# Row statistics one batch ahead, and V pieces 0 and 1 in the places of K pieces 6 and 7, in a gated cross-attention and mixture-of-experts block

## The chip, the cores and the metric

One core of a Trainium2 chip runs the whole program. The metric is device time in microseconds (us) of one execution, as the median of several runs. Engines are named PE (TensorE, matrix products), DVE (VectorE), ACT (ScalarE), POOL (GpSimd) and SP (SyncE, which here issues most DMAs).

## What is computed

x has 8 batches of 512 rows of 256, the context 8 batches of 1601 rows of 256.

```python
x = x + tanh(g_xattn) * xattn(layernorm(x), ctx, ctx)
x = x + tanh(g_ffn) * ffn(layernorm(x))

# xattn: 16 heads of 16; note the softmax over the queries (axis 2)
qh, kh, vh = heads(q @ Wq.T), heads(k @ Wk.T), heads(v @ Wv.T)
attn = softmax(einsum('bhnc,bhlc->bhnl', qh * 256 ** -0.5, kh), axis=2)
attn = attn / attn.sum(-1, keepdims=True)
out = einsum('bhnl,bhlc->bhnc', attn, vh) ... @ Wo.T

# ffn: top 2 of 8 experts, 256 -> 1024 (gelu) -> 256, weighted by the normalised router probabilities
```

## The kernel before

The program has two stages: attention with routing, batch by batch, and then the experts over 71 blocks of 128 routed rows. The change touches the first alone.

**Steps and units.** The 16 heads form four groups (g) of four, the 1601 context rows 13 tiles of up to 128 (the last has 65). A step s is one tile of one group, 52 steps a batch; its two units (p = 0, 1) have two heads each. For each unit PE makes scores, transposed, with the context rows on partitions and 512 queries in the columns (L732, `unit_scores`), DVE takes the negated maximum over the queries (L1114), ACT makes two exponentials with their sums (L934). There are three slots of scores in PSUM (`SLOTS`): a unit's scores wait for the exponentials of the unit three before. Per step DVE then inverts the four sums (L1100, `reciprocals`), POOL scales the tile of V by them (L1337), and PE multiplies three steps later (L745, `weigh`). At a turn of groups DVE takes the accumulator (L1104).

**Q and K in three parts.** Q and K are used in 16-bit parts: each projected piece is split into a high part (ACT, L870, `take`), a residual (DVE, L1009), a middle and a low part (POOL, L1389 and L1381, the low one a step later). The three parts of a piece lie in `parts`, a pair of buffers that pieces use in turn (`c % 2`), and SP stores them to DRAM (`store_parts`, Q on L445, K on L450). From there SP loads the stacks of a group of heads, 16 DMAs for each (`load_stacks`, L407 and L412). `ORDER` is the order in which the ten pieces of a batch are made and stored: K 0 to 7, then Q 0 and 1. K pieces 0 to 3 and Q 0 serve groups 0 and 1, K 4 to 7 and Q 1 groups 2 and 3. Before ACT writes a piece into its buffer it waits until the piece two before has been stored:

```python
wait(act, parts_stored[c % 2], (b * (CHUNKS // 2) + at // 2) * 16)   # at: the piece's place in ORDER
```

V pieces need none of this: ACT copies them once (L879) and DVE has no part in them.

**The order around the change.** The work beside the scores stands in tables by step (`FILL_AT`, for batch 0 `FIRST_BATCH_FILL_AT`): "next" pieces are projections of the batch after, "tail" those that finish the batch before (its last attention turn, the output projection, the routing), "cur" the batch's own. All share one PSUM bank, `spare`, so a piece starts on PE only when the one before has been taken. PE starts half of a K, Q or V piece a step early. ACT takes its part at the beginning of the step in front of the step's exponentials, DVE its part of Q and K at the end of the step. SP's program is one sequence: it waits for a piece's parts, issues, and goes on. `load_x` and `load_ctx` fetch x and the context two batches ahead, once their buffers are free (L461 after step 28, L466 after step 47).

**Statistics of x.** The layer norm of the next batch's x takes four row statistics on DVE (L1143, at `STATS_X`, steps 7 and 11 to 13), four aggregates (L1147, step 16), and POOL's normalising from step 17 (`CENTRE_X`). The statistics of x2 for the routing (L1133, L1137) stand at steps 10 to 12.

Of the kernel before, what the change touches and what calls it, by code (L numbers as in the profile page):

```python
# [41 lines left out]
KC = D // P  # L42
NT = N // P
LT = (L + P - 1) // P
GH = 4
G = H // GH
STEPS = G * LT
UNITS = 2 * STEPS
# [5 lines left out]
KCHUNK = 4  # L54
# [14 lines left out]


FILL_AT = {
    1: ("next", "k", 0), 3: ("next", "k", 1), 4: ("tail", "o_turn", 3), 5: ("tail", "attn_turn", 1),
    7: ("tail", "out_proj", 0), 9: ("tail", "out_proj", 1), 11: ("next", "k", 2), 13: ("next", "k", 3),
    15: ("next", "k", 4), 17: ("next", "k", 5), 18: ("cur", "o_turn", 0), 19: ("tail", "row_turn", 0),
    20: ("tail", "row_turn", 1), 22: ("tail", "logits", 0), 24: ("next", "k", 6), 26: ("next", "k", 7),
    27: ("next", "x_turn", 0), 28: ("next", "x_turn", 1), 30: ("next", "q", 0),
    32: ("next", "q", 1), 33: ("cur", "o_turn", 1), 35: ("next", "v", 0), 37: ("next", "v", 1), 38: ("tail", "prefix", 0),
    40: ("next", "v", 2), 42: ("next", "v", 3), 44: ("next", "v", 4), 46: ("next", "v", 5),
    47: ("next", "v", 6), 48: ("cur", "attn_turn", 0), 49: ("cur", "o_turn", 2),
}  # L80
# [5 lines left out]
FIRST_BATCH_FILL_AT = {  # L86
    1: ("cur", "own_v", 3), 3: ("cur", "own_v", 4), 5: ("cur", "own_v", 5), 6: ("cur", "own_v", 6),
    11: ("next", "k", 0), 13: ("next", "k", 1), 15: ("next", "k", 2), 17: ("next", "k", 3), 18: ("cur", "o_turn", 0),
    20: ("next", "k", 4), 22: ("next", "k", 5), 24: ("next", "k", 6), 26: ("next", "k", 7),
    27: ("next", "x_turn", 0), 28: ("next", "x_turn", 1), 30: ("next", "q", 0),  # L90
    32: ("next", "q", 1), 33: ("cur", "o_turn", 1), 35: ("next", "v", 0), 37: ("next", "v", 1), 39: ("next", "v", 2), 41: ("next", "v", 3),
    43: ("next", "v", 4), 44: ("cur", "o_turn", 2), 46: ("next", "v", 5), 47: ("next", "v", 6),
    48: ("cur", "attn_turn", 0),
}
# [7 lines left out]
LAG = 3  # L102
WARM_TURNS = 24
WARM_ROUTING, WARM_PLACED, WARM_EXPERTS, WARM_ROWS = 40, 60, 24, 18
ORDER = [KC + i for i in range(KC * KCHUNK)] + list(range(KC))
LOGITS = 22
ROUTE = 25
PLACE = 39
OUT = 9
STATS_X = (7, 11, 12, 13)  # L110
CENTRE_X = 17


class Iteration:
# [65 lines left out]
def wait_apart(eng, sem, value, passed):  # L180


    eng.wait_ge(sem, value)
    eng.sem_inc(passed, 1)
# [27 lines left out]
def attention_and_routing(nc, ctx, block, keep, x, ctx_t, g_xattn, g_ffn, wq_t, wk_t, wv_t, wo_t, router_t,  # L212
# [227 lines left out]
    def _(sp):  # L440
# [50 lines left out]
        def run(it):  # L491
            b = it.b
            if b == 0:

                sp.wait_ge(fill_taken, it.made("own_v", VF - 1))
                sp.dma_start(ctx_sb[:, :, :], ctx_rows[1]).then_inc(ctx_loaded, 16)
                stored_early(sp, ("q", 1), *(("k", i) for i in range(KCHUNK, 2 * KCHUNK)))
                load_stacks(0, 2)
            if it.cur and b > 0:

                wait(sp, scores_ready, b * UNITS)
                load_stacks(b, 3)
            if it.next:

                for g in range(G):
                    wait(sp, stack_in[g], stacks_by(b, g))
                for c in ORDER[0:KCHUNK]:
                    store_parts(it, c)
            if it.tail:
                sp.wait_ge(fill_taken, it.made("out_proj", 1))  # L510
                sp.dma_start(out_rows[b - 1], x2[:, :, :]).then_inc(x2_stored, 16)
            if it.next:
                for c in ORDER[KCHUNK:2 * KCHUNK]:
                    store_parts(it, c)
            if b == 0:
                load_stacks(0, 3)
            if it.cur:
                if it.tail:

                    wait_apart(sp, x2_stored, b * 16, passed_sp)  # L520
                    wait_apart(sp, rows_ready, 2 * b, passed_sp)
                sp.dma_start(x2[:, :, :], x_rows[b]).then_inc(x2_loaded, 16)
            if it.ahead:
                load_x(it)
            if it.next:
                stores = CHUNKS // 2 * 16
                store_parts(it, 0)
                wait_apart(sp, parts_stored[0], (b + 1) * stores, passed_sp)
                wait_apart(sp, parts_stored[1], (b + 1) * stores - 16, passed_sp)
                sp.wait_ge(scores_ready, b * UNITS + 2 * LT)  # L530
                load_stacks(b + 1, 0)
                store_parts(it, 1)
                wait_apart(sp, parts_stored[1], (b + 1) * stores, passed_sp)
                for g in range(1, G - 1):
                    sp.wait_ge(scores_ready, b * UNITS + (g + 1) * 2 * LT)
                    load_stacks(b + 1, g)
            if it.ahead:
                load_ctx(it)

# [39 lines left out]
    def _(pe):  # L579
# [63 lines left out]
        def fill(it, name, i, halves):  # L643
            b = it.b
            if 0 not in halves:
                pass
            elif name != "logits":

                wait(pe, fill_taken, it.made(name, i) - 1)
            if name == "x_turn":  # L650

                pe.wait_ge(xn_ready, 2 * (b + 2))
                mm = turn_x(spare, i)
            elif name == "q":
                mm = project_q(spare, i, halves)
            elif name == "k":
                if i == 0 and 0 in halves:
                    pe.wait_ge(ctx_loaded, (b + 1) * 16)
                mm = project_k(spare, i, halves)
            elif name in ("v", "own_v"):  # L660
                if (name, i) == ("own_v", len(EARLY_COPIED) - KC) and 0 in halves:

                    pe.wait_ge(early_copied, len(EARLY_COPIED))
                mm = project_v(spare, i, halves)
            elif name == "o_turn":

                pe.wait_ge(acc_taken, b * G + i + 1 if i < G - 1 else b * G)
                for t in range(NT):
                    mm = pe.transpose(spare[:, t * P:(t + 1) * P], o_acc[:, t * P:(t + 1) * P], ident[:, :])
            elif name == "attn_turn":  # L670
                for t in range(NT):
                    mm = pe.transpose(spare[:, t * P:(t + 1) * P], attn[:, t, i * P:(i + 1) * P], ident[:, :])
            elif name == "out_proj":
                if i == 0:
                    pe.wait_ge(wo_in, 32)
                for t in (2 * i + h for h in halves):
                    for k in range(KC):
                        mm = pe.matmul(spare[:, (t % 2) * D:(t % 2 + 1) * D], attn_t[:, k, t * P:(t + 1) * P],
                                       wo_sb[:, k, :], start=(k == 0), stop=(k == KC - 1))
            elif name == "row_turn":  # L680

                pe.wait_ge(rows_ready, 2 * b)
                for t in range(NT):
                    mm = pe.transpose(spare[:, t * P:(t + 1) * P], routed_rows[:, 0, t, i * P:(i + 1) * P], ident[:, :])
            elif name == "logits":
                for t in range(NT // 2, NT):
                    for k in range(KC):
                        mm = pe.matmul(spare[:, t * E:(t + 1) * E], row_t[:, k, t * P:(t + 1) * P],
                                       router_sb[:, k, :], start=(k == 0), stop=(k == KC - 1))
            elif name == "pads":  # L690
                mm = pe.matmul(spare[:, 0:E], ones[:, :], seen[:, :], start=True, stop=True)
            else:

                pe.wait_ge(route_step, b * ROUTE_STEPS)
                pe.matmul(spare[:, 0:NT * E], tri[:, :], chosen[:, :, :], start=True, stop=False)
                mm = pe.matmul(spare[:, 0:NT * E], ones[:, :], seen_at[:, :, :], start=False, stop=True)
            if 1 in halves:
                mm.then_inc(fill_ready, 1)
# [246 lines left out]
    def _(dve):  # L945
# [160 lines left out]
        def run(it):  # L1106
            b = it.b
            for s in range(STEPS):
                for p in range(2):
# [24 lines left out]
                    if p == 1 and it.tail and s == OUT + 3:  # L1134
                        wait_apart(dve, stats2_done, b * NT, passed_dve)
                        for t in range(NT):
                            dve.bn_aggr(mv2[:, t, :], stats2[:, t, :]).then_inc(mv2_ready, 1)  # L1137
                    if p == 0 and it.next and s in STATS_X:

                        t = STATS_X.index(s)  # L1140
                        if t == 0:
                            dve.wait_ge(x_loaded, (b + 2) * 16)
                        dve.bn_stats(stats1[:, t, :], x_in[:, t, :]).then_inc(stats_done, 1)  # L1143
                    if p == 1 and it.next and s == CENTRE_X - 1:
                        wait_apart(dve, stats_done, (b + 2) * NT, passed_dve)
                        for t in range(NT):
                            dve.bn_aggr(mv1[:, t, :], stats1[:, t, :]).then_inc(mv_ready, 1)  # L1147
                    if it.tail and s == ROUTE and p == 0:
# [540 lines left out]
```

## Time and profile before

| | |
|---|---|
| median of 3 runs | 1795.29 us |
| lowest, highest | 1794.12, 1796.07 us |
| the profiled execution: its own time | 1794.36 us |
| its span on the core | 1792.6 us |
| mean granted clock of TensorE | 0.996 |
| first exponential of batch 0, 1, 7 | 31.34, 180.59, 1088.38 us |

A profile is of one execution. Its span runs from the first to the last profiled instruction, and its time lies 1.8 us above. Times in the views are microseconds from the span's start. Busy time of an engine is the union of its instructions. The chain of waits follows the work back from the last instruction to whatever released each step, so it names the engine that set the pace in a stretch.

### The profile page before, as it was taken

How to read it: one execution, taken by the hardware profiler on the slowest of the kernel's cores; microseconds unless marked ns; L12 is line 12 of the kernel's file. 1: busy time of each engine (PE TensorE's matmuls, PEld its weight loads, DVE VectorE, ACT ScalarE, POOL GpSimd, SP SyncE). 2: the span in 40 equal slices, each digit the busy share in tenths (PEclk: the TensorE clock that was granted, in tenths of full speed). 3: DMA queues.
4: the chain of work that ended last, by engine and by line, in shares of the span. 5: the costliest groups of instructions: out<-in, count | busy, mean ns of one | idle time of the engine just before them, and what ended most of it. 6: DMA issues, size and time to landing. Idle time of an engine off the chain costs nothing.

```text
span 1792.6 us, 31795 instructions
## 1 busy us (share of the span) xinstructions
PE 1703.8 (95%) x10074; PEld 918.3 (51%) x10074; DVE 1417.2 (79%) x2293; ACT 1283.0 (72%) x3653; POOL 538.2 (30%) x821
## 2 busy tenths in 40 slices
PE   8999999999999999999999999889999999999997
PEld 5233334333333433333333342225899999999997
DVE  7998999999999999999999999997344444444442
ACT  5999999999999999999999999996111111111111
POOL 3331252352343225235223422213122222222222
PEclk9999999999999999999999999999999999999999
DMA  8546226414712721551371163419222222222221
GB/s 231 139 121 183 66 70 158 129 40 123 187 47 62 198 72 52 158 154 40 102 187 51 51 172 75 154 52 326 67 37 35 36 37 35 38 35 35 36 37 27
DMA packets 128247, 172.90 MB, mean 96 GB/s; under 512 B 14496, under 2 KB 105760, under 8 KB 128128
## 3 DMA queue, kind: packets, MB, share of 16 engines
q1 hardware_dynamic: 113152, 150.51, 30.8%
q0 software_dynamic: 14144, 20.44, 6.6%
q8 instruction: 54, 0.88, 0.2%
q14 instruction: 65, 0.53, 0.1%
q10 hardware_dynamic: 832, 0.53, 0.1%
HBM read 117.96 MB, written 53.47 MB: 96 GB/s over the span
## 4 chain that ended last, share of the span: by engine, by line
ACT 40%; PE 30%; DVE 20%; issue 7%; DMA 2%; POOL 1%; SPq 0%; POOLq 0%; DVEq 0%; ACTq 0%
ACT w_all L934 37%; DVE negmax L1114 14%; PE scores L1507 14%; PE scores L1520 13%; ACT w_all L879 1%; ACT parts L870 1%; DVE resid L1009 1%; DMA out<-row_t,gate_token 1%; PE spare L1497 1%; DVE rz L1100 1%; PE scores L732 1%; PE spare L593 1%; DVE x L1025 1%; DVE stats L1133 1%; DVE stats L1143 0%
## 5 line engine op out<-in xcount | busy, mean ns | idle before, releaser
L934 ACT ACTIVATE w_all<-scores,negmax 128x512 f32<-128x512 f32 (+1 forms) x1664 | 1128.9, 778 | 19.9 <-DVE negmax L1114 15.4
L1114 DVE TENSOR_REDUCE negmax<-scores 128x2 f32<-128x1024 f32 (+1 forms) x832 | 1001.9, 1215 | 53.8 <-PE scores L732 47.4
L732 PE MATMUL scores<-q_stack,w_all 128*128 128x512 bf16 (+1 forms) x1664 | 532.9, 385 | 42.1 <-ACT w_all L934 34.3
L934 ACT ACTIVATION_READ_ACCUMULATOR w_all<-scores,negmax 128x1 f32 (+1 forms) x1664 | 495.2, 298 | 0.0
L745 PE MATMUL acc<-w_all,vz 128*32 128x512 f32 (+1 forms) x3328 | 443.7, 605 | 0.0
L732 PEld LDWEIGHTS scores<-q_stack,w_all 128*128 128x128 bf16 (+1 forms) x1664 | 136.8, 99 | 575.2 <-ACT w_all L934 514.6
L1553 ACT ACTIVATE projections<-scores 128x512 f32<-128x512 f32 x142 | 84.8, 597 | 445.8 <-PE scores L1507 440.2
L1337 POOL TENSOR_TENSOR vz<-w_all,rz 128x68 f32<-128x68 f32 (+1 forms) x416 | 124.5, 299 | 776.3 <-DVE rz L1100 751.0
L1507 PEld LDWEIGHTS scores<-row_t,q_stack 128*128 128x128 f32 x2272 | 264.4, 192 | 7.0 <-issue 2.0
L1507 PE MATMUL scores<-row_t,q_stack 128*128 128x128 f32 x2272 | 265.6, 275 | 1.9 <-DVE row_t L1580 1.9
L1520 PE MATMUL scores<-room,projections 128*128 128x256 f32 x1136 | 256.8, 379 | 0.0
L1633 POOL DMA_INDIRECT out<-row_t,gate_token x71 | 120.3, 1694 | 407.9 <-DVE row_t L1593 374.3
L1520 PEld LDWEIGHTS scores<-room,projections 128*128 128x128 f32 x1136 | 210.4, 190 | 25.7
L1586 DVE COPY gate_token<-parts 128x2 f32<-128x2 f32 x71 | 12.0, 169 | 186.3 <-DMA out<-row_t,gate_token 186.3
L745 PEld LDWEIGHTS acc<-w_all,vz 128*32 128x32 f32 (+1 forms) x3328 | 65.6, 108 | 138.1 <-issue 121.9
L593 PE MATMUL spare<-w_all,projections 128*128 128x400 f32 (+1 forms) x228 | 97.7, 511 | 10.2 <-DVE resid L1009 10.2
L1593 DVE TENSOR_SCALAR row_t<-scores,gate_token 128x256 f32<-128x256 f32 x71 | 34.4, 484 | 88.0 <-PE scores L1520 88.0
L601 PE MATMUL spare<-projections,w_all 128*128 128x256 f32 (+1 forms) x400 | 103.1, 381 | 0.1
L1570 DVE COPY q_stack<-w_all 128x2048 f32 x71 | 86.9, 1225 | 6.4 <-issue 1.8
L1575 DVE COPY room<-w_all 128x2048 f32 x71 | 86.5, 1218 | 0.0
L601 PEld LDWEIGHTS spare<-projections,w_all 128*128 128x128 f32 (+1 forms) x400 | 73.6, 186 | 19.8 <-ACT w_all L879 3.3
L1100 DVE RECIPROCAL rz<-z 128x4 f32<-128x4 f32 (+1 forms) x416 | 69.7, 167 | 2.1 <-ACT w_all L934 2.1
(215 smaller groups left out, 1048.9 us busy)
## 6 DMA issues: line engine op xcount, KB each, us to landing
w_all<-k_parts SPq DMA_DIRECT2D x248, 200.1 KB, 3.5
w_all<-in_w SPq DMA_DIRECT2D x16, 1024.0 KB, 10.0
q_stack<-q_parts SPq DMA_DIRECT2D x248, 64.0 KB, 3.3
k_parts<-parts SPq DMA_DIRECT2D x42, 300.0 KB, 2.9
w_all<-in_ctx_t SPq DMA_DIRECT2D x7, 1601.0 KB, 7.1
parts<-routed SPq DMA_DIRECT2D x71, 129.0 KB
q_parts<-parts SPq DMA_DIRECT2D x14, 384.0 KB, 3.9
routed<-pad_row SPq DMA_DIRECT2D x8, 645.0 KB
```

Source lines behind the costliest of these rows:

```text
L593: mm = pe.matmul(bank[:, 0:KCOLS[c + 1] - KCOLS[c]], wk_sb[:, k, m * P:(m + 1) * P], ctx_sb[:, k, KCOLS[c]:KCOLS[c + 1]], start=(k == 0), ...
L601: mm = pe.matmul(bank[0:r, (lt % 2) * D:(lt % 2 + 1) * D], ctx_sb[:, k, lt * P:lt * P + r], wv_sb[:, k, :], start=(k == 0), stop=(k == KC ...
L732: mm = pe.matmul(scores[0:r, 2 * (u % SLOTS) + j % 2, :], k_stacks[g][:, j, lt * P:lt * P + r], q_stack[:, g, j, :], start=True, stop=True)
L745: mm = pe.matmul(acc[32 * j:32 * j + 32, :], vz[0:r, s % RING, j, :], probs[0:r, s % RING, j, :], start=(lt == 0), stop=(lt == LT - 1))
L934: act.activation(probs[0:r, s % RING, j, :], scores[0:r, 2 * (u % SLOTS) + j % 2, :], ACT.Exp, bias=negmax[0:r, u % 4, j % 2:j % 2 + 1], a ...
L1100: dve.reciprocal(rz[0:r, s % RING, :], z[0:r, s % RING, :]).then_inc(rz_ready, 1)
L1114: dve.tensor_reduce(negmax[0:r, u % 4, :], scores[0:r, 2 * (u % SLOTS):2 * (u % SLOTS) + 2, :], AX.X, ALU.max, negate=True).then_inc(negma ...
L1337: pool.tensor_tensor(vz[0:r, s % RING, :, 0:DH + 1], v_ones[b % 2][0:r, lt, g * GH:(g + 1) * GH, :], rz[0:r, s % RING, :].unsqueeze(2).to_ ...
L1507: mm = pe.matmul(ps_hidden[:, slot * BANKS + h // HB, (h % HB) * BLK:(h % HB + 1) * BLK], w1_sb[:, slot, k * HID + h * P:k * HID + (h + 1) ...
L1520: mm = pe.matmul(ps_y[:, slot, 0:D], hidden[:, slot, h * BLK:(h + 1) * BLK], w2_sb[:, slot, h * D:(h + 1) * D], start=(h == 0), stop=(h == ...
L1570: dve.tensor_copy(w1_sb[:, slot, :], w1_all[:, bass.ds(e * (KC * HID), KC * HID)]).then_inc(w1_ready, 1)
L1633: pool.indirect_dma_start(out=out, out_offset=bass.IndirectOffsetOnAxis(gate_token[:, slot, 1:2].bitcast(U32), 0), in_=result[:, slot, :], ...
```

## The change

Five things change, all in the first stage:

- In `FILL_AT` V 0 and V 1 take steps 1 and 3, K 0 to K 5 move to steps 11, 13, 15, 17, 24 and 26, and K 6 and K 7 stand at 35 and 37. In batch 0 the K pieces up to K 5 stay and V 0, V 1 (steps 24, 26) change places with K 6, K 7 (steps 35, 37).
- `ORDER` becomes K 0 to 5, Q 0, Q 1, K 6, K 7.
- SP stores K 6 behind Q 1 and in front of the loads of stack 1, and K 7 between the loads of stacks 1 and 2.
- The wait for the context goes from K 0 to V 0.
- From batch 1 on the statistics of x have been made one batch earlier, at steps 43 to 46, with the aggregates at step 47 (`STATS_AHEAD`). Batch 0 has both its own, at the old steps, and those for batch 2's x. Their number stays.

```diff
--- before.py
+++ after.py
@@ -69,12 +69,12 @@
 
 
 FILL_AT = {
-    1: ("next", "k", 0), 3: ("next", "k", 1), 4: ("tail", "o_turn", 3), 5: ("tail", "attn_turn", 1),
-    7: ("tail", "out_proj", 0), 9: ("tail", "out_proj", 1), 11: ("next", "k", 2), 13: ("next", "k", 3),
-    15: ("next", "k", 4), 17: ("next", "k", 5), 18: ("cur", "o_turn", 0), 19: ("tail", "row_turn", 0),
-    20: ("tail", "row_turn", 1), 22: ("tail", "logits", 0), 24: ("next", "k", 6), 26: ("next", "k", 7),
+    1: ("next", "v", 0), 3: ("next", "v", 1), 4: ("tail", "o_turn", 3), 5: ("tail", "attn_turn", 1),
+    7: ("tail", "out_proj", 0), 9: ("tail", "out_proj", 1), 11: ("next", "k", 0), 13: ("next", "k", 1),
+    15: ("next", "k", 2), 17: ("next", "k", 3), 18: ("cur", "o_turn", 0), 19: ("tail", "row_turn", 0),
+    20: ("tail", "row_turn", 1), 22: ("tail", "logits", 0), 24: ("next", "k", 4), 26: ("next", "k", 5),
     27: ("next", "x_turn", 0), 28: ("next", "x_turn", 1), 30: ("next", "q", 0),
-    32: ("next", "q", 1), 33: ("cur", "o_turn", 1), 35: ("next", "v", 0), 37: ("next", "v", 1), 38: ("tail", "prefix", 0),
+    32: ("next", "q", 1), 33: ("cur", "o_turn", 1), 35: ("next", "k", 6), 37: ("next", "k", 7), 38: ("tail", "prefix", 0),
     40: ("next", "v", 2), 42: ("next", "v", 3), 44: ("next", "v", 4), 46: ("next", "v", 5),
     47: ("next", "v", 6), 48: ("cur", "attn_turn", 0), 49: ("cur", "o_turn", 2),
 }
@@ -86,9 +86,9 @@
 FIRST_BATCH_FILL_AT = {
     1: ("cur", "own_v", 3), 3: ("cur", "own_v", 4), 5: ("cur", "own_v", 5), 6: ("cur", "own_v", 6),
     11: ("next", "k", 0), 13: ("next", "k", 1), 15: ("next", "k", 2), 17: ("next", "k", 3), 18: ("cur", "o_turn", 0),
-    20: ("next", "k", 4), 22: ("next", "k", 5), 24: ("next", "k", 6), 26: ("next", "k", 7),
+    20: ("next", "k", 4), 22: ("next", "k", 5), 24: ("next", "v", 0), 26: ("next", "v", 1),
     27: ("next", "x_turn", 0), 28: ("next", "x_turn", 1), 30: ("next", "q", 0),
-    32: ("next", "q", 1), 33: ("cur", "o_turn", 1), 35: ("next", "v", 0), 37: ("next", "v", 1), 39: ("next", "v", 2), 41: ("next", "v", 3),
+    32: ("next", "q", 1), 33: ("cur", "o_turn", 1), 35: ("next", "k", 6), 37: ("next", "k", 7), 39: ("next", "v", 2), 41: ("next", "v", 3),
     43: ("next", "v", 4), 44: ("cur", "o_turn", 2), 46: ("next", "v", 5), 47: ("next", "v", 6),
     48: ("cur", "attn_turn", 0),
 }
@@ -102,13 +102,15 @@
 LAG = 3
 WARM_TURNS = 24
 WARM_ROUTING, WARM_PLACED, WARM_EXPERTS, WARM_ROWS = 40, 60, 24, 18
-ORDER = [KC + i for i in range(KC * KCHUNK)] + list(range(KC))
+EARLY_K = 6
+ORDER = [KC + i for i in range(EARLY_K)] + list(range(KC)) + [KC + i for i in range(EARLY_K, KC * KCHUNK)]
 LOGITS = 22
 ROUTE = 25
 PLACE = 39
 OUT = 9
 STATS_X = (7, 11, 12, 13)
 CENTRE_X = 17
+STATS_AHEAD = (43, 44, 45, 46)
 
 
 class Iteration:
@@ -510,7 +512,7 @@
                 sp.wait_ge(fill_taken, it.made("out_proj", 1))
                 sp.dma_start(out_rows[b - 1], x2[:, :, :]).then_inc(x2_stored, 16)
             if it.next:
-                for c in ORDER[KCHUNK:2 * KCHUNK]:
+                for c in ORDER[KCHUNK:EARLY_K]:
                     store_parts(it, c)
             if b == 0:
                 load_stacks(0, 3)
@@ -525,15 +527,19 @@
             if it.next:
                 stores = CHUNKS // 2 * 16
                 store_parts(it, 0)
-                wait_apart(sp, parts_stored[0], (b + 1) * stores, passed_sp)
-                wait_apart(sp, parts_stored[1], (b + 1) * stores - 16, passed_sp)
+                wait_apart(sp, parts_stored[0], (b + 1) * stores - 16, passed_sp)
+                wait_apart(sp, parts_stored[1], (b + 1) * stores - 32, passed_sp)
                 sp.wait_ge(scores_ready, b * UNITS + 2 * LT)
                 load_stacks(b + 1, 0)
                 store_parts(it, 1)
+                store_parts(it, KC + EARLY_K)
+                sp.wait_ge(scores_ready, b * UNITS + 4 * LT)
+                load_stacks(b + 1, 1)
+                store_parts(it, KC + EARLY_K + 1)
+                wait_apart(sp, parts_stored[0], (b + 1) * stores, passed_sp)
                 wait_apart(sp, parts_stored[1], (b + 1) * stores, passed_sp)
-                for g in range(1, G - 1):
-                    sp.wait_ge(scores_ready, b * UNITS + (g + 1) * 2 * LT)
-                    load_stacks(b + 1, g)
+                sp.wait_ge(scores_ready, b * UNITS + 6 * LT)
+                load_stacks(b + 1, 2)
             if it.ahead:
                 load_ctx(it)
 
@@ -658,6 +664,8 @@
                     pe.wait_ge(ctx_loaded, (b + 1) * 16)
                 mm = project_k(spare, i, halves)
             elif name in ("v", "own_v"):
+                if (name, i) == ("v", 0) and 0 in halves:
+                    pe.wait_ge(ctx_loaded, (b + 1) * 16)
                 if (name, i) == ("own_v", len(EARLY_COPIED) - KC) and 0 in halves:
 
                     pe.wait_ge(early_copied, len(EARLY_COPIED))
@@ -1135,14 +1143,24 @@
                         wait_apart(dve, stats2_done, b * NT, passed_dve)
                         for t in range(NT):
                             dve.bn_aggr(mv2[:, t, :], stats2[:, t, :]).then_inc(mv2_ready, 1)
-                    if p == 0 and it.next and s in STATS_X:
+                    if p == 0 and b == 0 and s in STATS_X:
 
                         t = STATS_X.index(s)
                         if t == 0:
                             dve.wait_ge(x_loaded, (b + 2) * 16)
                         dve.bn_stats(stats1[:, t, :], x_in[:, t, :]).then_inc(stats_done, 1)
-                    if p == 1 and it.next and s == CENTRE_X - 1:
+                    if p == 1 and b == 0 and s == CENTRE_X - 1:
                         wait_apart(dve, stats_done, (b + 2) * NT, passed_dve)
+                        for t in range(NT):
+                            dve.bn_aggr(mv1[:, t, :], stats1[:, t, :]).then_inc(mv_ready, 1)
+                    if p == 1 and it.ahead and s in STATS_AHEAD:
+
+                        t = STATS_AHEAD.index(s)
+                        if t == 0:
+                            dve.wait_ge(x_loaded, (b + 3) * 16)
+                        dve.bn_stats(stats1[:, t, :], x_in[:, t, :]).then_inc(stats_done, 1)
+                    if p == 1 and it.ahead and s == STATS_AHEAD[-1] + 1:
+                        wait_apart(dve, stats_done, (b + 3) * NT, passed_dve)
                         for t in range(NT):
                             dve.bn_aggr(mv1[:, t, :], stats1[:, t, :]).then_inc(mv_ready, 1)
                     if it.tail and s == ROUTE and p == 0:
```

**SP around the store of Q 1, in batch 1.** Names: `q_parts` and `k_parts` are in DRAM, `parts` is the pair of buffers, `q_stack` and `w_all` (the room that holds K's stacks) are the stacks. Before:

```order
L407 DMA q_stack<-q_parts 16x4x512
L412 DMA w_all<-k_parts 16x4x1601
L445 DMA q_parts<-parts 128x3x512 [waits parts_ready]
L407 DMA q_stack<-q_parts 16x4x512 [waits parts_stored_1,scores_ready]
L412 DMA w_all<-k_parts 16x4x1601
```

And with the change:

```order
L409 DMA q_stack<-q_parts 16x4x512
L414 DMA w_all<-k_parts 16x4x1601
L447 DMA q_parts<-parts 128x3x512 [waits parts_ready]
L452 DMA k_parts<-parts 128x3x400 [waits parts_ready]
L409 DMA q_stack<-q_parts 16x4x512 [waits scores_ready]
L414 DMA w_all<-k_parts 16x4x1601
```

The 16 loads of stack 0 stand in front of Q 1's store as before; K 6's store comes in behind it, and the loads of stack 1 no longer wait for Q 1's store to land.

**DVE in batch 1, steps 11 and 12.** Before:

```order
L1100 RECIPROCAL rz<-z 128x4
L1009 SCALAR_TENSOR_TENSOR resid<-spare,parts 128x400
L1133 BN_STATS stats<-x 128x6 x2
L1114 TENSOR_REDUCE negmax<-scores 65x2
L1143 BN_STATS stats<-room 128x6
L1114 TENSOR_REDUCE negmax<-scores 65x2
L1100 RECIPROCAL rz<-z 128x4
L1137 BN_AGGR mv<-stats 128x2 x4
```

And with the change:

```order
L1108 RECIPROCAL rz<-z 128x4
L1017 SCALAR_TENSOR_TENSOR resid<-spare,parts 128x400
L1141 BN_STATS stats<-x 128x6 x2
L1122 TENSOR_REDUCE negmax<-scores 65x2 x2
L1108 RECIPROCAL rz<-z 128x4
L1145 BN_AGGR mv<-stats 128x2 x4
```

The statistics of x between the two reductions of step 12 are gone; the residual at step 11 is K 0's now and was K 2's.

## Rows read from the trace of the kernel before

**Rows 1.** The page, part 1

```profile
PE 1703.8 (95%) x10074; PEld 918.3 (51%) x10074; DVE 1417.2 (79%) x2293; ACT 1283.0 (72%) x3653; POOL 538.2 (30%) x821
```

**Rows 2.** Busy time by batch: 0 and 1 (columns in its first row)

```profile
core 0: us, PE busy (x) PEld busy (x) DVE busy (x) ACT busy (x) POOL busy (x), PEclk, DMA share, GB/s
31.34:180.59 149.25, 141.11 (x746) 47.82 (x745) 138.59 (x183) 148.60 (x439) 38.80 (x77) 1.00 0.62 156
180.59:331.89 151.30, 143.80 (x797) 51.20 (x797) 144.84 (x234) 148.64 (x436) 54.29 (x94) 1.00 0.38 107
```

**Rows 3.** Same view: batch 1 in two parts, batch 7's steps 0 to 20

```profile
180.59:242.72 62.13, 58.50 (x328) 20.09 (x327) 61.06 (x97) 59.88 (x174) 29.00 (x47) 1.00 0.23 67
242.72:331.89 89.17, 85.30 (x474) 31.11 (x471) 83.77 (x138) 88.76 (x264) 25.29 (x48) 1.00 0.49 135
1088.38:1146.94 58.56, 54.48 (x306) 16.57 (x305) 56.80 (x83) 56.83 (x169) 13.57 (x29) 0.97 0.39 123
```

**Rows 4.** Chain that ended last, batch 1, early (start us, us, what)

```profile
200.59 0.66 DVE x L1025
201.25 0.33 DVE stats L1143
...
217.61 0.26 DVE mv L1137 x4
...
226.26 0.47 DVE resid L1009
```

**Rows 5.** Same view, batch 1, late

```profile
250.97 0.39 ACT parts L870
...
274.95 3.95 ACT w_all L934 x12
...
288.89 0.47 ACT w_all L879
```

**Rows 6.** Timeline, batch 1, ACT (start us, us, engine, line, operation, tiles)

```profile
268.39 0.74 ACT L870 ACTIVATE parts<-spare 128x512 bf16<-128x512 f32 x1
...
282.94 0.58 ACT L879 COPY w_all<-spare 128x512 f32<-128x512 f32 x1
...
288.72 0.65 ACT L879 COPY w_all<-spare 128x512 f32<-128x512 f32 x1
```

**Rows 7.** Timeline, batch 1, SP's queue

```profile
274.00 0.37 SPq L445 DMA_DIRECT2D q_parts<-parts  x1
276.65 0.54 SPq L407 DMA_DIRECT2D q_stack<-q_parts  x1
...
287.67 0.58 SPq L445 DMA_DIRECT2D q_parts<-parts  x1
291.86 0.53 SPq L407 DMA_DIRECT2D q_stack<-q_parts  x1
```

**Rows 8.** Line L445, the store issued at 287.67

```profile
DMA to landing us min/median/max: 4.1/4.1/4.1
```

**Rows 9.** Timeline, batch 0: twice SP's queue, once ACT

```profile
98.91 11.79 SPq L450 DMA_DIRECT2D k_parts<-parts  x3
...
122.69 0.37 SPq L445 DMA_DIRECT2D q_parts<-parts  x1
...
137.25 0.79 ACT L879 COPY w_all<-spare 128x512 f32<-128x512 f32 x1
```

**Rows 10.** Timeline, batch 1, PE at the start of step 38

```profile
289.19 0.62 PE L732 MATMUL scores<-q_stack,w_all 128*65 128x512 bf16 x2
```

**Rows 11.** Busy time around two batch borders (granted clock after POOL)

```profile
1085.16:1088.57 3.41, 1.97 (x12) 0.55 (x12) 1.95 (x4) 3.00 (x11) 1.29 (x2) 1.00 0.72 158
1088.57:1091.99 3.42, 3.42 (x16) 0.55 (x12) 2.05 (x3) 2.60 (x8) 0.29 (x1) 0.50 0.95 251
328.60:332.00 3.40, 2.45 (x14) 0.85 (x14) 1.94 (x4) 2.99 (x11) 1.28 (x2) 1.00 0.69 158
```

**Rows 12.** Timeline, ACT, batch 7's first step

```profile
1092.39 0.69 ACT L934 ACTIVATE w_all<-scores,negmax 128x512 f32<-128x512 f32 x1 [1.22 <-DVE negmax L1114]
```

## The prediction

> **What bounds the kernel now.** The page's busy times come first [rows 1]: PE at 95%, DVE 79%, ACT 72% over the span say little, since the attention stage and the expert stage behind it have different limits. The busy time by batch is next [rows 2]: a batch is 52 steps of four exponentials each; batch 0 takes 149.25 us and a middle batch (1 to 6; 180.59 to 1088.38 [rows 2, 3] is six times 151.30) 151.30, with ACT busy 148.6 of it. That looks like a batch on ACT alone, but two parts behave differently [rows 3]. In steps 0 to 20 of batch 1 (62.13 us) DVE is busy 61.06 and ACT leaves 2.25 idle; in steps 21 to 51 (89.17) ACT is busy 88.76 and DVE has 5.4 free. The chain confirms it: early it runs through DVE's reductions, row statistics and residuals [rows 4], late through ACT's exponentials, six in 3.95 us, or 2.63 a step, and its copies of finished pieces [rows 5]. So DVE work taken out of the early stretch pays, and DVE work put into the late one is free up to its 5.4 us; a wait of ACT in the late stretch is paid in full. The experts are not touched.
>
> **Early stretch, batches 1 to 6.** Four row statistics of x leave it at 0.33 us each on the chain, four aggregates at 0.26 together [rows 4], and two K residuals (K 0, K 1) at 0.47 each: 4 x 0.33 + 0.26 + 2 x 0.47 = 2.52 us of DVE. In steps 1 and 3 ACT now copies V, 0.47 where K took 0.39 [rows 5], so ACT's work there grows by 0.16. If DVE bounds every moment, 2.5 us are saved. The nearest row for what waits remain is batch 7, whose early stretch has neither pieces of a next batch nor statistics of x: 58.56 us [rows 3], less 1.22 that it waits at its start in a lowered clock [rows 12], is 57.3. To it come ACT's four K copies (1.56) and two V copies (0.94), and four times the 0.08 by which a residual on DVE is longer than its copy on ACT: 57.3 + 2.5 + 0.3 = 60.1, or **2.0 us saved**, which I take, as it is built from a stretch with the same leftover work. The least is 1.4: statistics and aggregates alone (1.58) less the 0.16, with K's share lost to PE, which has eight short products for a V piece in a stretch where its scores are wanted at once. Batch 0 keeps its early statistics and has K and V where they were up to step 22; V at 24 and 26 costs it 0.16.
>
> **Late stretch.** The statistics ahead (1.58) and two residuals (0.94) are 2.5 us of DVE against 5.4 free [rows 3]: nothing, covered by ACT's exponentials; should they bunch before the turn at step 49, 0.3. V pieces 0 and 1 need the context at step 0, as K 0 did; it is loaded behind the same piece (V 6), so nothing moves there. The store of x2 goes behind K 3 at step 18 instead of 14, and the x2 load stays behind K's store at step 27; its reader is in the next batch.
>
> **The queue, which decides it.** K 6 and K 7 are now pieces 8 and 9 of ten and use the two buffers after Q 0 and Q 1. ACT may write K 7 at step 37 only when Q 1's store has landed. SP reaches that store only after the 16 loads of stack 0, as before; before, nobody but SP waited for it. In the trace: Q 0's store issues at 274.00, lands, the loads start at 276.65, Q 1's store issues at 287.67 [rows 7] and needs 4.1 us to land [rows 8]; SP itself goes on at 291.86 [rows 7]. ACT stands at its copy of step 37 at 288.72 [rows 6]. K 6 at step 35 (282.94) finds Q 0 long stored. All these times hang on Q 0's copy at 268.39 [rows 6], in both kernels, so ACT waits 291.8 - 288.7 = 3.1 us; K 7's copy is 0.08 shorter than V 1's: **3.0 us lost per batch**. Behind ACT's wait stand its exponentials of step 37, DVE's residual and PE's next piece, so all engines stop. DVE's and PE's lead, three units of scores, is full by then and buys nothing, since ACT is the bound after it too.
>
> Batch 0: Q 0's store now finds an empty queue, because stack load 3 follows K 5 (stored at 98.91) and not K 7. It issues at 122.69 [rows 9], plus 2.65 to the loads, plus 11.02 for them [rows 7], plus 4.1: 140.5, against ACT's copy at 137.25 [rows 9]: 3.2 lost, less 0.08.
>
> **The clock.** While ACT waits, PE has issued the scores of step 38 (done by 289.8 [rows 10]) and stops until K 7's residual is done, about 292.8 (291.8 + 0.39 + 0.47): 3 us idle. In batch 7's start PE was busy for 1.97 of 3.41 us, and in the next 3.42 us its granted clock was 0.50, the lower of its two levels (1.2 against 2.4 GHz), while at batch 2's border with 2.45 of 3.40 busy it stayed up [rows 11]. A gap of 3 us will mostly be the lower kind. It cost 1.22 us there, where PE had no lead [rows 12]; here three units of scores are ready, so I take **0.5** per batch, between 0 (no fall) and 1.2. [...]
>
> **Sum.** Batches 1 to 6: -2.0 + 3.0 + 0.5 = +1.5, six times +9.0. Batch 0: 0.16 + 3.1 + 0.5 = +3.8. Batch 7 has none of it. +12.8 us on the profiled execution's 1794.36 gives 1807.2; that execution is 0.9 below the median 1795.29, so 1808.1 against the median: **1808**.
>
> **Rivals.** (a) *Q 1's store lands fast.* Its 4.1 us come from the loads before it; Q 0's, in an empty queue, needed at most 2.65 [rows 7]. Then the wait is 1.5 and the clock stays: 6 x (-2.0 + 1.5) + 1.8 = -1, or 1794, no change. Against it: the same loads precede the store as before, and K 6's store and stack load 1 now follow at once. The Trainium skill (DMA: Bandwidth & Descriptors, Anatomy of one DMA) puts a transfer at about 2.0 us plus its size over 436 GB/s, by an estimate 2.9 us for these 384 KB, which would take 1.2 us off each of seven waits and give 1800; that fit is for the other issue path, and the row shows 4.1. 12%. (b) *ACT doesn't wait*: faster. If the store landed by 288.7, one us after issue, the change would do what its early stretch gives, 6 x -2.0 = -12, or 1783. For it speaks only that my reading of the buffer counts could be wrong, or that DVE and not ACT sets step 37 (it has 5.4 us free in the stretch). 7%. (c) *V on PE and a full clock price*: the early gain is 1.4 and the clock costs 1.2: 6 x 2.8 + 4.5 = +21, or 1817. 15%. (d) *No clock fall and the whole early gain*: 6 x 0.5 + 3.3 = +6, or 1801.6, still slower. 16%. The forecast itself: 50%.
>
> **Numbers.** A measurement of this kernel can tell about 0.2% (3.6 us) from no change. Slower by more: forecast, (c) and (d), 81%, less a little for a (d) with a shorter landing: 0.80. Within: (a), 0.13. Faster: (b), 0.07. The range holds the forecast, (c) nearly to its end, and (d) with up to 4 us of quicker landings: 1798 to 1816.
>
> **What would show it.** Right: a wait of about 3 us before ACT's K copy at step 37 in batches 0 to 6, with Q 1's store landing just before it; a lower granted clock after most of them; steps 0 to 20 of a middle batch near 60.1 us; batch 0 at 153, middle batches at 152.8, batch 7 at 141.3. Wrong: a middle batch below 151 us (no wait, or the early gain above 2.5), Q 1's store landing within 3 us, or DVE bound at steps 43 to 51.

## The result, and the profile after

The changed kernel takes 1814.23 us (median of 5 runs, 1812.34 to 1817.07) against 1795.29 of the kernel before: a ratio of 1.0103, with a 95% interval of 1.0089 to 1.0117. It is 18.9 us slower. The prediction said 1808, between 1798 and 1816, and slower.

Part 1 of its page, which answers to [rows 1]; the span is 1810.6 us, 18.0 more than before:

```profile
PE 1709.2 (94%) x10074; PEld 921.3 (51%) x10074; DVE 1414.2 (78%) x2293; ACT 1281.2 (71%) x3653; POOL 538.3 (30%) x821
```

Busy time stayed within a few us on every engine, so the loss is waiting. The view by batch shows where; its rows are batches 0, 1, 2 and 7 and, last, steps 0 to 20 of batch 2:

```profile
core 0: us, PE busy (x) PEld busy (x) DVE busy (x) ACT busy (x) POOL busy (x), PEclk, DMA share, GB/s
31.42:184.80 153.38, 143.10 (x750) 49.40 (x750) 138.96 (x191) 149.25 (x440) 38.99 (x78) 0.99 0.59 153
184.80:339.37 154.57, 144.58 (x797) 51.51 (x797) 144.37 (x234) 148.12 (x436) 54.32 (x94) 0.99 0.38 105
339.37:493.08 153.71, 144.70 (x797) 51.54 (x798) 144.38 (x234) 148.21 (x437) 54.26 (x94) 0.99 0.41 106
1107.25:1247.40 140.15, 126.58 (x712) 34.83 (x712) 135.59 (x217) 139.58 (x417) 30.91 (x68) 1.00 0.40 121
339.37:399.96 60.59, 58.51 (x334) 21.38 (x333) 59.01 (x87) 59.27 (x175) 25.52 (x43) 1.00 0.23 62
```

Batch 0 went from 149.25 to 153.38, a middle batch from 151.30 [rows 2] to 154.57 and 153.71 (the six are 153.74 in the mean, from 184.80 to 1107.25). ACT is busy no longer in a middle batch (148.1 us in batch 1 against 148.6), and 0.65 us longer in batch 0. The early stretch is shorter, as meant: 60.59 against 62.13 [rows 3]. Batch 7 lost nothing, and gained 1.1 (141.27 us before by the same measure, from its first exponential to the end of the last).

ACT's waits in the changed kernel say it in one line (engine, line, what was waited for: us in total, times, the longest):

```profile
ACT parts L878 <- DMA q_parts<-parts: 19.7, 7, 3.6
```

Seven waits for Q 1's store, 19.7 us; the kernel before had none of this kind. The first of a middle batch is the longest of the seven (the others are 2.3 to 3.3 us). In the timeline of ACT (K 7's high part at step 37, then an exponential of step 39):

```profile
295.10 0.51 ACT L878 ACTIVATE parts<-spare 128x401 bf16<-128x401 f32 x1 [3.65 <-DMA q_parts<-parts]
...
301.83 0.69 ACT L942 ACTIVATE w_all<-scores,negmax 128x512 f32<-128x512 f32 x1 [0.90 <-DVE negmax L1122]
```

SP's queue around it, which answers to [rows 7]: Q 0's store, Q 1's store behind the 16 loads, K 6's store.

```profile
276.66 0.37 SPq L447 DMA_DIRECT2D q_parts<-parts  x1
...
289.87 0.58 SPq L447 DMA_DIRECT2D q_parts<-parts  x1
291.09 0.36 SPq L452 DMA_DIRECT2D k_parts<-parts  x1
```

And the chain of waits there (start us, us, what):

```profile
289.22 0.59 SPq L414
...
289.87 5.16 DMA q_parts<-parts
...
295.10 0.52 ACT parts L878
...
295.71 0.59 DVE resid L1017
...
296.35 0.41 PE spare L703 x2
...
297.10 0.85 PE scores L740 x2
297.96 1.87 PE acc L753 x8
```

From Q 0's store to Q 1's are 13.2 us, as before (13.67); the landing takes 5.16 here, and 3.9 to 4.6 in the other six batches. Read down the chain: loads, store, ACT's high part, DVE's residual, PE's next piece, its scores and its weighing. Between 292.4 and 295.0 PE, DVE and ACT did nothing at all and POOL worked 0.28 us: they had stopped behind this one store. What PE did:

```profile
291.49 0.62 PE L740 MATMUL scores<-q_stack,w_all 128*65 128x512 bf16 x2
296.35 0.41 PE L703 MATMUL spare<-chosen,tri 128*128 128x32 f32 x2 [4.24 <-DVE resid L1017]
...
296.92 1.04 PE L740 MATMUL scores<-q_stack,w_all 128*65 128x512 bf16 x2
297.89 1.94 PE L753 MATMUL acc<-w_all,vz 128*32 128x512 f32 x8
...
300.46 1.06 PE L753 MATMUL acc<-w_all,vz 128*32 128x512 f32 x8
```

It stood idle for 4.24 us, and then its weighing took 1.94 us where the next one takes 1.06. The granted clock (the number after POOL's) in a stretch of 3.4 us behind each of the seven waits:

```profile
143.00:146.40 3.40, 3.40 (x10) 2.26 (x9) 2.18 (x4) 3.40 (x11) 1.21 (x3) 0.52 0.98 205
296.80:300.20 3.40, 3.40 (x14) 0.66 (x13) 2.02 (x4) 3.40 (x13) 1.24 (x3) 0.51 0.96 206
450.40:453.80 3.40, 3.40 (x14) 0.83 (x14) 2.14 (x4) 3.40 (x12) 1.14 (x3) 0.51 1.00 206
604.00:607.40 3.40, 3.40 (x12) 0.42 (x11) 1.78 (x4) 3.40 (x11) 1.39 (x3) 0.51 0.64 166
757.80:761.20 3.40, 3.40 (x15) 1.03 (x15) 2.25 (x4) 3.40 (x11) 0.94 (x3) 0.54 0.97 198
911.30:914.70 3.40, 3.40 (x14) 0.89 (x15) 2.13 (x4) 3.40 (x12) 1.06 (x3) 0.52 1.02 207
1065.00:1068.40 3.40, 3.40 (x16) 0.40 (x19) 1.70 (x4) 3.40 (x11) 1.31 (x3) 0.54 1.00 207
```

It is at or close to 0.50, the lower level, all seven times, each time behind the idle stretch; before, it was down once in the attention stage [rows 11].

### The profile page after: what moved, and what is told of

Its sections match the earlier page's. It is cut to its first block, busy times and chain, and to the rows that moved or that the text cites. A ratio compares the mean times of both kernels' runs of the same rounds, so it can differ in the third digit from the quotient of the medians.

```text
span 1810.6 us, 31809 instructions
## 1 busy us (share of the span) xinstructions
PE 1709.2 (94%) x10074; PEld 921.3 (51%) x10074; DVE 1414.2 (78%) x2293; ACT 1281.2 (71%) x3653; POOL 538.3 (30%) x821
## 4 chain that ended last, share of the span: by engine, by line
PE 39%; ACT 34%; DVE 13%; issue 6%; SPq 4%; DMA 4%; POOL 0%; DVEq 0%; POOLq 0%; ACTq 0%
ACT w_all L942 31%; PE scores L1525 14%; PE scores L1538 13%; DVE negmax L1122 10%; PE acc L753 4%; PE scores L740 4%; DMA q_parts<-parts 2%; SPq L414 2%; SPq L409 2%; ACT w_all L887 1%; PE spare L686 1%; DVE resid L1017 1%; ACT parts L878 1%; PE spare L1515 1%; SPq L405 1%
## 5 line engine op out<-in xcount | busy, mean ns | idle before, releaser
L942 ACT ACTIVATION_READ_ACCUMULATOR w_all<-scores,negmax 128x1 f32 (+1 forms) x1664 | 464.8, 279 | 0.0
L1407 POOL TENSOR_TENSOR parts<-resid,zero 128x400 bf16<-128x400 f32 (+1 forms) x70 | 62.3, 890 | 31.5 <-DVE resid L1017 31.0
```

Source lines behind the costliest of these rows:

```text
L942: act.activation(probs[0:r, s % RING, j, :], scores[0:r, 2 * (u % SLOTS) + j % 2, :], ACT.Exp, bias=negmax[0:r, u % 4, j % 2:j % 2 + 1], a ...
```

## The experiments

The theory at this point: ACT's wait for Q 1's store, with the lowered clock behind it, is the whole loss, and the early stretch gives what it measured. The rival: the work that moved to the end of the batch (two residuals, the statistics) is too much for DVE there. In all kernels here the numbering of pieces and the semaphores are those of the changed kernel unless said. Each was timed beside the kernel before, whose own median was 1792.8 us in the first four experiments and 1794.3 in the last three, not 1795.29. So differences between kernels are taken from the ratios, in microseconds of 1795.29, and not from the medians.

### Q 1's store between the loads

```diff
         def load_stacks(b, g, at=None, between=None):
             for blk in range(BLOCKS):
+                if blk == at:
+                    between()
...
-                load_stacks(b + 1, 0)
-                store_parts(it, 1)
+                load_stacks(b + 1, 0, 3, lambda: store_parts(it, 1))
```

> The changed kernel, but SyncE stores Q 1 after three of the eight pairs of stack 0's loads instead of after all eight. Theory (ACT's wait at step 37 for Q 1's store, with the clock's fall behind it, is the whole loss): Q 1's parts are ready about 3.8 us after stack 0's loads begin, the store issues 7 us earlier and lands some 4 us before K 7 needs its buffer. No wait of ACT there, no lowered clock at step 38, a middle batch near 149.7 us (151.3 less the 1.6 of the early stretch), about 1786 us in all (1784 to 1788). Rival (K's residuals and the statistics are too much for DVE late in the batch, and the store's wait only shows it): it stays within 4 us of 1814, with waits for DVE at steps 35 to 49 instead.

Measured: 1781.43 us, ratio 0.9936 (0.9922 to 0.9949), which is 11.5 us faster than the kernel before (1783.8 where that takes 1795.29). Its batch 1, the early stretch of it, and batch 7:

```profile
180.36:329.95 149.59, 143.10 (x797) 51.24 (x797) 144.28 (x234) 147.76 (x436) 54.30 (x94) 1.00 0.39 108
180.36:240.96 60.60, 58.38 (x333) 21.34 (x332) 59.02 (x87) 59.17 (x174) 25.50 (x43) 1.00 0.19 59
1077.80:1217.89 140.09, 126.53 (x712) 34.78 (x711) 135.59 (x217) 139.52 (x417) 30.91 (x68) 1.00 0.39 123
```

Q 1's store in SP's queue, and ACT's K 7 copy in batch 1, with no wait before it:

```profile
279.28 0.58 SPq L447 DMA_DIRECT2D q_parts<-parts  x1
```

```profile
286.86 0.57 ACT L879 ACTIVATE parts<-spare 128x401 bf16<-128x401 f32 x1
```

The store issues 7.05 us behind Q 0's (272.23) and not 13.2. All seven waits are gone and the clock isn't lowered in the attention stage. A middle batch is 149.59 us, as expected (149.7); the total by the ratio is 2 us below the middle of the expectation and 0.2 outside its range, and 1.1 of that is batch 7's. The rival falls: the residuals at steps 35 and 37 and the statistics at 43 to 47 are all still there.

### Each half alone

The statistics of x ahead in the kernel before (no change of pieces), and the change of pieces with the statistics at their old steps:

```diff
-                    if p == 0 and it.next and s in STATS_X:
+                    if p == 0 and b == 0 and s in STATS_X:
...
+                    if p == 1 and it.ahead and s in STATS_AHEAD:
```

> The kernel before, with the statistics of x one batch ahead and nothing else of the change. If DVE bounds all of the early stretch, six middle batches lose the 1.58 us of statistics and aggregates each: 1795.3 - 9.5 = 1785.8. If only steps 11 to 16, where they stood in a crowd, pay: about 1 us a batch, 1789. Rival (DVE has no room for them at steps 43 to 47): part or all comes back there, 1792 or more. No wait of ACT for a store in any case.

> The change without the statistics ahead: V 0 and 1 in the places of K 6 and 7 alone. Theory: early gain 0.3 to 0.8 us in six batches, wait of 3 us and clock of 1.2 us in seven: 1795.3 - 3 + 29 - 1 (no clock fall into batch 7, if the phase falls so) = about 1820 (1817 to 1823). The two halves add up to the change if e2 is near 1788. Rival (statistics late in the batch are what hurts, through DVE): below 1805.

Measured: the statistics alone 1785.80, ratio 0.9964 (0.9951 to 0.9978), or -6.5 us; the pieces alone 1818.88, ratio 1.0141 (1.0125 to 1.0157), or +25.3. Together they make +18.8, the change made +18.5 by its ratio: the halves add up. (The 1785.80 is the first answer's 1785.8 by chance: the kernel before took 1792.8 beside it, and 6.5 us is what the second answer says.) Batch 2 and its early stretch with the statistics ahead alone:

```profile
330.92:481.29 150.37, 143.49 (x797) 51.17 (x798) 144.46 (x234) 148.25 (x437) 54.27 (x94) 1.00 0.39 108
330.92:392.12 61.20, 58.20 (x328) 20.07 (x327) 59.78 (x89) 59.49 (x174) 29.02 (x47) 1.00 0.24 70
```

61.20 against 62.13: 0.9 us of the 1.58 taken off DVE come through, the second of the two answers. Nothing comes back late in the batch. Batch 2 with the pieces alone, a stretch within its early part, and the whole early stretch of batch 3:

```profile
340.67:496.12 155.45, 146.75 (x797) 51.54 (x796) 144.82 (x234) 149.13 (x436) 54.44 (x94) 0.98 0.38 105
386.90:390.10 3.20, 3.20 (x12) 0.42 (x10) 1.96 (x7) 2.21 (x7) 3.12 (x6) 0.52 0.27 96
496.13:557.68 61.55, 58.93 (x334) 21.41 (x333) 60.35 (x95) 59.83 (x175) 25.57 (x43) 1.00 0.23 61
```

In batch 2 the clock fell a second time, in steps 16 and 17, as it did in batches 1 and 5; their early stretches take 63.1 to 63.2 us. Batches 3, 4 and 6 have no such fall and take 61.55, so the fall cost 1.6. It was not expected, and why it came in some batches only isn't settled. Against 62.13, 61.55 is a gain of 0.6 for the pieces alone, and with the 0.9 of the statistics it makes the 1.5 of the change.

That the totals add up to within 0.3 us is in part luck, since the pieces alone have three falls more than the change, some 5 us. In the batches without a second fall the halves make -0.9 and +3.1 a middle batch, together +2.2, where the change has +2.4.

### PE fed during the wait

```diff
                 if it.cur:
                     unit_scores(it.b, s, 0)
+                if it.next and s == 3 * LT - 1:
+                    for _ in range(14):
+                        pe.matmul(acc[:, 0:P], pad_row[:, 0:P], ident[:, :], start=False, stop=False)
```

> The changed kernel, and in batches 0 to 6 PE makes 14 products with weights of zero into the running accumulator behind the first unit of step 38, where it stood idle during ACT's wait; they add zero and nobody waits for them. ACT's wait stays. Theory (the 1.2 us at steps 38 and 39 are the lowered clock): the granted clock stays up, these steps lose their excess, 1814 - 6 x 1.2 - 0.8 = about 1806 (1804 to 1809). Rival (they are the restart of a pipeline that ran dry, whatever the clock): no change or slower by what the products themselves delay, 1813 to 1820.

Measured: 1801.12, ratio 1.0047 (1.0033 to 1.0061), some 10 us below the change by their ratios. ACT's waits stay. Below them stand a stretch of batch 1 that follows the wait, and batches 1 to 6 together:

```profile
ACT parts L881 <- DMA q_parts<-parts: 17.9, 7, 2.9
```

```profile
292.40:302.00 9.60, 9.20 (x60) 4.19 (x62) 8.43 (x16) 9.60 (x29) 2.58 (x5) 1.00 0.80 197
182.79:1096.71 913.92, 878.36 (x4921) 326.14 (x4922) 865.60 (x1396) 888.05 (x2617) 325.63 (x564) 1.00 0.38 105
```

The granted clock is 1.00, and it isn't lowered behind any of the seven waits. Batches 1 to 6 take 152.32 us in the mean against 153.74, which is 1.4 less; 0.2 of it is a shorter wait (2.6 in the mean of ACT's gaps before the K copy, 2.8 in the change). So about 1.2 us of each middle batch were the clock's. The rival, a refill whatever the clock, has no part left: steps 38 and 39 of batch 2 together take 5.76 us, exactly as in the kernel with the store between the loads, and 7.01 in the change. Seven times 1.2 and 1.8 of shorter waits (19.7 to 17.9 in all) make the 10 us; the expectation had only the clock's part.

### The store later, and first

```diff
-                store_parts(it, 1)
-                store_parts(it, KC + EARLY_K)
                 sp.wait_ge(scores_ready, b * UNITS + 4 * LT)
-                load_stacks(b + 1, 1)
+                load_stacks(b + 1, 1, 2, lambda: (store_parts(it, 1), store_parts(it, KC + EARLY_K)))
```

> The changed kernel, with Q 1's store (and K 6's behind it) moved two pairs of loads later, into stack 1's loads: four issues of 0.64 us, 2.6 us. Theory (ACT waits for this store's landing, microsecond for microsecond): the wait of some 3 us becomes 5.5 to 6, seven times, and the clock falls as often as before: 1.0103 + 7 x 2.6 / 1795 = ratio 1.020, about 1832 (1829 to 1838, the upper end if the longer idle time of PE holds the clock down longer). Rival (part of the wait is DVE's or PE's own lateness, which the store's would then cover): less than half of that, below 1823.

Measured: 1832.62, ratio 1.0224 (1.0208 to 1.0239). ACT's waits:

```profile
ACT parts L878 <- DMA q_parts<-parts: 39.7, 7, 6.4
```

Four more issues ahead of the store are 7 x 2.6 = 18 us by count, and the waits grew by 20.0 of the 21.7 us by which this kernel is slower than the change (by the ratios). So each microsecond that the store is late costs one. The clock was lowered at all seven waits again, but for twice as long. A stretch of 6.8 us around the first wait of a middle batch:

```profile
298.40:305.20 6.80, 3.27 (x14) 1.25 (x14) 3.20 (x5) 4.51 (x14) 0.85 (x1) 0.54 1.07 259
```

It is near 0.50 for the whole stretch in all seven batches, where the change had 3.4 us of it. That doubling cost little. A middle batch takes 156.96 us in the mean; less the 149.57 of the kernel with the store between the loads and 5.5 of waiting, 1.9 are left, against 1.4 in the change (153.74 less 149.57 and 2.8). PE was busy for only 3.27 us of the 6.8, so part of the lowered time passed while it stood idle.

> The changed kernel, with Q 1's store ahead of all of stack 0's loads, which therefore wait some 4 us for Q 1's parts. Theory: who stores Q 1 before ACT needs the buffer is free in the rest; stacks 0 to 2 arrive 4 us later, tens of microseconds before they are read, so no wait shows and the time is that of the store between the loads: ratio 0.992 to 0.995, 1781 to 1787. Rival (the loads' start matters, for the queue is then busy when the context's load or K 6's store comes): 0.996 or more.

The edit is that of the first experiment with a 0 in place of the 3. Measured: 1782.34, ratio 0.9938 (0.9923 to 0.9954), the same as between the loads within the interval. Its batch 3:

```profile
480.24:629.81 149.57, 140.74 (x782) 51.21 (x798) 144.28 (x234) 147.84 (x437) 54.27 (x94) 1.00 0.42 109
```

149.57 us, equal to the other's. Stack 0's loads can wait 4 us and nobody sees it; the store can't. This run also shows what the 16 loads do to the landing. Q 1's store in batch 1, from issue to landing:

```profile
DMA to landing us min/median/max: 2.6/2.6/2.6
```

It is 2.6 or 2.7 us in six of the seven batches and 4.5 in one; behind the loads the same store took 3.9 to 5.2 in the change.

### What the early stretch keeps

Of the 2.5 us taken off DVE 1.5 came through. In the chain of the kernel with Q 1's store between the loads, batch 2 at step 11:

```profile
362.09 0.17 DVE rz L1109
362.26 0.46 DVE resid L1018
362.72 0.66 DVE stats L1142 x2
363.38 1.13 DVE negmax L1123
```

Behind the inverted sums, which wait for ACT, stand a residual and two statistics of x2, 1.12 us, ahead of the reduction that ACT needs next. ACT waits 0.67 us. The last experiment keeps the work and changes its place:

```diff
-                    if p == 1 and it.tail and s in (OUT + 1, OUT + 2):
-                        for t in range(2 * (s - OUT - 1), 2 * (s - OUT)):
-                            dve.bn_stats(stats2[:, t, :], x2[:, t, :]).then_inc(stats2_done, 1)
+                    if it.tail and s in (OUT + 1, OUT + 2):
+                        t = 2 * (s - OUT - 1) + p
+                        dve.bn_stats(stats2[:, t, :], x2[:, t, :]).then_inc(stats2_done, 1)
```

> The kernel with Q 1's store between the loads, and the four statistics of x2 at steps 10 and 11 one behind each reduction instead of two at the step's end. Theory (what the early stretch has left over its ACT work comes where DVE has a pile of work between the inverted sums and the next reduction: 0.46 + 0.66 us behind them at step 11, and ACT waits 0.7 us): the wait at step 11 falls by 0.3 us and more in six or seven batches, 2 to 4 us in all, ratio 0.991 to 0.993. Rival (DVE's sum of work there decides, not its place): no difference from the store between the loads, 0.9936.

Measured: 1780.45, ratio 0.9929 (0.9917 to 0.9941). The exponential at step 12 in the kernel with the store between the loads, and in this one:

```profile
364.54 0.68 ACT L943 ACTIVATE w_all<-scores,negmax 65x512 f32<-65x512 f32 x1 [0.67 <-DVE negmax L1123]
```

```profile
364.06 0.68 ACT L943 ACTIVATE w_all<-scores,negmax 65x512 f32<-65x512 f32 x1 [0.39 <-DVE negmax L1123]
```

The wait fell by 0.28 us and the early stretch by 0.24, so its place does count, but a middle batch is only 0.14 shorter (149.43 from 149.57). The rest is lost in hundredths over the late steps, and no run shows why. The expected 2 to 4 us are not there by the trace, which has 0.9, and the two intervals overlap, so by time it isn't told from the simpler version.

## Why the prediction was right, and where it was off

**The queue, which decides it: right.** The wait was to come at step 37, in batches 0 to 6, for Q 1's store behind the loads of stack 0, 3.1 us a middle batch. It came there, seven times, and cost 19.7 us, 2.8 on average; taking the store out from behind the loads removed it, putting it further back made it longer by as much. The landing was forecast at 4.1 us from one row and took 3.9 to 5.2, 4.4 in the mean.

**The clock: right in kind, mis-sized.** The sum had 0.5 us a batch, "between 0 (no fall) and 1.2", with three ready units of scores as the reason for the low end. The fall came seven times out of seven and cost 1.2 in a middle batch, the value of [rows 12]. The step that failed is that lead: the units ready were used up in the first 4 us of ACT's work, and PE, at half rate, was by then behind with the scores of step 39, where ACT waited 0.90 us. Over seven falls that is 4.9 us. The Trainium skill (TensorE: Matmul & The Clock Gate, Part 1) has the throttled clock as the default state, which activity releases; the seven rows above, each at the lower level behind PE's idle stretch, agree with it.

**The early stretch: too large a gain.** 2.0 us were taken, 1.5 measured (62.13 to 60.59), at the low end of the 1.4 to 2.5 given. What failed is the use of batch 7 for the leftover waits: it has no K residual beside the statistics of x2 at step 11. ACT's wait behind the pile there is 0.67 us in a middle batch and 0.19 in batch 7, which is the 0.5 that the forecast lacked. Six batches, 2.8 us.

**Batch 7: missed.** Its start was to be unchanged at 1.22 us of lowered clock; in the change the clock stayed up there and the batch took 1.1 less. Why it stayed up is open. **Late stretch, context, x2: right**, at nothing. **Batch 0: right**, 153.38 against 153; its early load of stack 3 did clear the queue for Q 0's store.

Summed over the span: six middle batches +2.44, or +14.6, batch 0 +4.1, batch 7 -1.1, together +17.6 of the span's 18.0, against +12.8 forecast. The misses are +4.9 for the clock, +2.8 for the early stretch, -2.0 for waits some 0.3 us shorter than forecast, and -1.1 for batch 7. Two of them happened to take back part of the others, and the measured 1814.23 lies near the end of the range.

Of the rivals, (a) and (b) had no part, since the store never landed within 3 us in its place. Rival (a) did see rightly that the landing is long because of the loads: with the store ahead of them it took 2.6. Rival (c), 1817, came nearest. Its clock price of 1.2 is the measured one and its early gain of 1.4 is close to 1.5, though not for its reason: the K pieces' share came through (0.6 of 0.78), and it is the statistics' share that was partly lost (0.9 of 1.58).

## What to carry to other kernels

When a piece of work is moved to a later place in a rotation of buffers, look at what must be *stored* before its buffer is free, and where in the issuing queue that store stands: a store that nobody waited for can sit behind any number of loads, and the first reader of its landing pays for all of them. Here three pairs of loads in front of it instead of eight turned +1.0% into -0.6%. And if the matrix engine stops during a wait, count the lowered clock at the full price that the trace shows for it; three units of scores ready ahead saved nothing of it here.

## What the runs showed of the hardware

In the changed kernel the border into batch 7 had PE as little busy as before (1.96 us of 3.40, against 1.97 of 3.41 in [rows 11]), and yet the clock did not fall there:

```profile
1103.80:1107.20 3.40, 1.96 (x12) 0.39 (x4) 2.08 (x3) 3.04 (x10) 1.38 (x3) 1.00 0.70 152
1107.20:1110.60 3.40, 3.40 (x23) 0.74 (x22) 3.06 (x5) 3.27 (x9) 0.29 (x1) 1.00 0.87 242
```

The kernel with the statistics ahead alone had PE busy there for the same 1.96 us, in as many instructions, and its clock did fall:

```profile
1079.30:1082.70 3.40, 1.96 (x12) 0.39 (x4) 2.05 (x3) 3.04 (x10) 1.29 (x3) 0.98 0.68 155
1082.70:1086.10 3.40, 3.40 (x13) 0.64 (x12) 1.66 (x4) 2.88 (x8) 0.29 (x1) 0.52 0.88 242
```

So PE's busy time ahead of a point didn't alone tell whether the clock falls. The landing of the same store, Q 1's behind the same loads, took 3.8 to 4.3 us in the seven batches of the kernel before and 3.9 to 5.2 in the change, with K 6's store and the next stack's loads issued at once behind it. That these lengthened it isn't shown, and the run with the store first speaks against it: 16 loads came at once behind the store there, and it took 2.6 or 2.7 us in six of seven batches. New in the changed kernel are also two short waits of ACT's K copies for an earlier K store, 0.8 us in all and 0.5 the longest. The store behind the longer one took 3.95 us to land, where the next two of that batch took 2.9; no run shows what held it up.
